# Gathers paced by their own landings instead of by pair products and mixes, in a recommendation tower on one core

## The reference

```python
e = jnp.stack([tbl_0[ids[:, 0]], ..., tbl_25[ids[:, 25]]], axis=1)
x = layer_norm(dense_t @ Wd.T, gd, bd)
y = layer_norm(jnp.einsum('bnd,ed->bne', sparse_t, Ws), gs, bs)
y = jnp.einsum('bne,pn->bep', y, Wsi)
y = layer_norm(y, gsi, bsi)
y = jnp.swapaxes(y, 1, 2)
T = jnp.concatenate([x[:, None, :], y], axis=1)
Z = jnp.einsum('bnd,bmd->bnm', T, T)
Zflat = Z[:, TRIL_I, TRIL_J]
out = layer_norm(Zflat @ Wl.T, gl, bl)
h = jnp.concatenate([z, r_dense_t], axis=1)
h = jnp.maximum(h @ W_top1 + b_top1, 0.0)
h = jnp.maximum(h @ W_top2 + b_top2, 0.0)
y = h @ W_top3
```

## Time and profile before

| | us |
|---|---|
| runs (3), median | 211.37 |
| runs, lowest to highest | 209.83 to 212.67 |
| the profiled execution's own time | 211.83 |
| its span, first to last instruction | 210.0 |

### The profile page before, as it was taken

One profiled execution on the slowest core, in us unless ns is written; L12 is line 12 of the kernel. 1 busy time (PEld: TensorE's weight loads), 2 busy tenths in 40 slices (PEclk: granted clock), 3 DMA queues, 4 the chain that ended last, 5 costly groups with the idle time before them and its releaser, 6 DMA issues.

```text
span 210.0 us, 4185 instructions
## 1 busy us (share of the span) xinstructions
PE 162.5 (77%) x1644; PEld 105.3 (50%) x1644; DVE 99.3 (47%) x192; ACT 88.5 (42%) x225; POOL 100.0 (48%) x113
## 2 busy tenths in 40 slices
PE   0593888683798795948986878579877969997996
PEld 0332635351355363726554637355555567465574
DVE  2463928635457655553072738260545574661011
ACT  2613235451164664541473436232644535642251
POOL 4777374667474664765546557736173710000000
PEclk9999589999599998596999999958999978999999
DMA  6713314172011144111101243101010630005100
GB/s 160 229 21 79 108 29 112 33 246 53 16 25 18 29 118 76 28 26 21 25 6 30 81 91 53 28 16 27 4 28 13 153 50 3 0 3 138 24 3 0
DMA packets 20260, 11.58 MB, mean 55 GB/s; under 512 B 12945, under 2 KB 17681, under 8 KB 20242
## 3 DMA queue, kind: packets, MB, share of 16 engines
q1 hardware_dynamic: 16226, 7.83, 14.2%
q0 software_dynamic: 3328, 3.41, 8.6%
q10 hardware_dynamic: 688, 0.08, 0.3%
HBM read 9.15 MB, written 2.16 MB: 54 GB/s over the span
## 4 chain that ended last, share of the span: by engine, by line
PE 63%; issue 19%; DVE 10%; DMA 4%; ACT 3%; SPq 0%; ACTq 0%; DVEq 0%
PE proj_ps L474 11%; PE mix_ps L440 10%; PE o_ps L490 8%; PE quad_ps L451 7%; PE dots_ps L465 6%; PE o_turn_ps L403 3%; PE o_turn_ps L528 2%; DVE var_p L881 2%; PE turn_ps L432 2%; PE o_ps L403 2%; DVE feats L905 2%; DVE e_prod L890 2%; DVE var_n L893 2%; PE o_ps L422 2%; PE dots_ps L396 2%
## 5 line engine op out<-in xcount | busy, mean ns | idle before, releaser
L373 POOL DMA_INDIRECT e_rows<-table_dram,rows_sb x104 | 99.1, 953 | 68.1 <-PE dots_ps L465 33.8
L890 DVE TENSOR_TENSOR e_prod<-quad_ps,e_rows 128x384 f32<-128x384 f32 (+1 forms) x16 | 9.5, 591 | 56.6 <-PE quad_ps L451 44.7
L465 PE MATMUL dots_ps<-feats 128*32 128x33 f32 x1024 | 19.1, 203 | 21.2 <-issue 20.8
L474 PE MATMUL proj_ps<-f_sb,proj_w 128*128 128x512 f32 x60 | 32.2, 619 | 1.3 <-DVE feats L905 0.6
L465 PEld LDWEIGHTS dots_ps<-feats 128*32 128x32 f32 x1024 | 14.6, 113 | 36.1 <-issue 35.0
L440 PE MATMUL mix_ps<-mixw_sb,e_unit 128*128 128x192 f32 (+4 forms) x128 | 26.7, 364 | 6.3 <-issue 5.1
L440 PEld LDWEIGHTS mix_ps<-mixw_sb,e_unit 128*128 128x128 f32 x128 | 24.8, 235 | 13.6 <-issue 9.9
L682 ACT COPY f_sb<-mix_ps 64x512 f32<-64x512 f32 x32 | 18.5, 579 | 20.1 <-PE mix_ps L440 16.4
L490 PE MATMUL o_ps<-wl_gained,z_pairs 128*128 128x512 f32 (+1 forms) x40 | 21.2, 664 | 0.5 <-DMA z_pairs<-z_dram 0.5
L451 PEld LDWEIGHTS quad_ps<-gram,e_cols 128*128 128x128 f32 x104 | 13.4, 194 | 16.3 <-issue 11.0
L881 DVE TENSOR_REDUCE var_p<-y_sq 128x16 f32<-128x512 f32 x32 | 20.5, 677 | 1.6 <-ACT y_sq L667 1.6
(11 more groups left out here) (142 smaller groups left out, 176.8 us busy)
## 6 DMA issues: line engine op xcount, KB each, us to landing
z_dram<-z_mine SPq DMA_DIRECT2D x4, 512.0 KB, 3.2
e_rows<-table_dram,rows_sb POOLq DMA_INDIRECT x104
w_sb<-w_dram SPq DMA_DIRECT2D x2, 512.0 KB
wl_sb<-wl_dram SPq DMA_DIRECT2D x2, 512.0 KB
w_sb<-w_dram SPq DMA_DIRECT2D x1, 768.0 KB
dense_sb<-dense_t_dram SPq DMA_DIRECT2D x1, 512.0 KB
wl_sb<-wl_dram SPq DMA_DIRECT2D x1, 256.0 KB
z_pairs<-z_dram SPq DMA_DIRECT2D x4, 64.0 KB, 2.1
```

The source lines that it names most:

```text
L373: pool.indirect_dma_start(out=e_rows[:, chunk, t, D * ab:D * (ab + 1)], out_offset=None, in_=table, in_offset=bass.IndirectOffsetOnAxis(ap ...
L465: mm = pe.matmul(dots_ps[PR * k:PR * (k + 1), (PR + 1) * g:(PR + 1) * (g + 1)], f[:, 2:PR + 2], f[:, 0:PR + 1], start=True, stop=True)
L474: pe.matmul(proj_of(s, ab), proj_w[:], f_sb[:, q % 2, ab, :], start=True, stop=True).then_inc(projected, 1)
L890: dve.tensor_tensor(e_prod[:, 0:2 * nt, :].rearrange("p a d -> p (a d)"), quad_ps[:, 0:P * nt], e_rows[:, chunk, t0:t0 + nt, :].rearrange( ...
```

## The change

The sixteen semaphores `gathered` are replaced by four, `landed`, that the gathers increment in turn: gather g (0 to 103) adds 16 to `landed[g % 4]` when it lands. Before gather g is issued, POOL waits until gather g-3 has landed, so that at most three are in flight. POOL waits for nothing else: `after_round` is gone, with its waits for `mixed`, `dotted` and earlier rows. Who needs a slot's rows (`turn` on PE, the four loads on SP) waits for all four semaphores to reach the count of that slot's last gather. DVE's wait in `variance_n` is dropped; it waits for `quad_done` there in any case.

```diff
+IN_FLIGHT = 3
+
+
+def gathers_up_to(s):
+
+    return sum(2 * tiles_of(slot % QUARTERS)[1] for slot in range(s + 1))
...
-        gathered = [[sem(f"gathered{chunk}_{q}") for q in range(QUARTERS)] for chunk in range(CHUNKS)]
+        landed = [sem(f"landed{k}") for k in range(IN_FLIGHT + 1)]
...
+        def rows_landed(eng, s):
+
+            number = gathers_up_to(s)
+            for k in range(IN_FLIGHT + 1):
+                eng.wait_ge(landed[k], 16 * ((number - 1 - k) // (IN_FLIGHT + 1) + 1))
...
             for q in range(3):
-                sp.wait_ge(gathered[0][q], 32 * tiles_of(q)[1])
+                rows_landed(sp, q)
...
-            sp.wait_ge(gathered[0][3], 32 * tiles_of(3)[1])
+            rows_landed(sp, 3)
...
-            def after_round(i):
-                if i >= 2:
-                    pool.wait_ge(dotted, i - 1)
-                elif i >= 0:
-                    pool.wait_ge(mixed, i + 1)
-                    pool.wait_ge(gathered[0][i + 1], 32 * tiles_of(i + 1)[1])
-
-            for chunk in range(CHUNKS):
-                for q in range(QUARTERS):
-                    after_round(chunk * QUARTERS + q - 2)
-                    t0, nt = tiles_of(q)
-                    for t in range(t0, t0 + nt):
-                        for ab in range(2):
-                            col = (chunk * TILES + t) * 2 + ab
-                            pool.indirect_dma_start(
...
-                            ).then_inc(gathered[chunk][q], 16)
+            for s in range(SLOTS):
+                chunk, q = place(s)
+                t0, nt = tiles_of(q)
+                for n in range(2 * nt):
+                    g = gathers_up_to(s) - 2 * nt + n
+                    if g >= IN_FLIGHT:
+                        older = g - IN_FLIGHT
+                        pool.wait_ge(landed[older % (IN_FLIGHT + 1)], 16 * (older // (IN_FLIGHT + 1) + 1))
+                    t, ab = t0 + n // 2, n % 2
+                    col = (chunk * TILES + t) * 2 + ab
+                    pool.indirect_dma_start(
...
+                    ).then_inc(landed[g % (IN_FLIGHT + 1)], 16)
...
-                pe.wait_ge(gathered[chunk][q], 32 * nt)
+                rows_landed(pe, s)
...
-                dve.wait_ge(gathered[chunk][q], 32 * nt)
```

More of the change, by code:

```diff
@@ L357, in _ @@
             pool.wait_ge(rows_ready, 1)
-            def after_round(i):
-                if i >= 2:
-                    pool.wait_ge(dotted, i - 1)
-                elif i >= 0:
-                    pool.wait_ge(mixed, i + 1)
-                    pool.wait_ge(gathered[0][i + 1], 32 * tiles_of(i + 1)[1])
-            for chunk in range(CHUNKS):
-                for q in range(QUARTERS):
-                    after_round(chunk * QUARTERS + q - 2)
-                    t0, nt = tiles_of(q)
-                    for t in range(t0, t0 + nt):
-                        for ab in range(2):
-                            col = (chunk * TILES + t) * 2 + ab
-                            pool.indirect_dma_start(
-                                out=e_rows[:, chunk, t, D * ab:D * (ab + 1)], out_offset=None, in_=table,
-                                in_offset=bass.IndirectOffsetOnAxis(ap=rows_sb[:, col:col + 1], axis=0),
-                            ).then_inc(gathered[chunk][q], 16)
+            for s in range(SLOTS):
[9 more added lines that the diff above has]
+                    pool.indirect_dma_start(
+                        out=e_rows[:, chunk, t, D * ab:D * (ab + 1)], out_offset=None, in_=table,
+                        in_offset=bass.IndirectOffsetOnAxis(ap=rows_sb[:, col:col + 1], axis=0),
+                    ).then_inc(landed[g % (IN_FLIGHT + 1)], 16)
         @block.tensor
```

## The result

The changed kernel takes **285.21 us** (median of 4 runs, 284.60 to 285.66), the kernel before 210.60 (4 runs, 209.75 to 212.67). The ratio is **1.352, with a 95% interval of 1.341 to 1.364**: 74.6 us slower, where 269 us was forecast with a range of 218 to 291. The profiled execution took 284.60 us with a span of 282.8. One thing for reading the runs further down: some executions come out 1.5 to 4% longer than the shortest of their kernel (three of four in e1, and of the kernel before two of seven beside e5 to e8 and five of seven beside e9 to e11), and e1 and the ratios are read from the others.

What follows compares the result with a forecast made beforehand. PE was taken to bound the kernel, stalling for instructions during gather bursts. Gathers landed at 135.1 us plus 132.0 us of rest gave 267.1 us of span, with 1.8 us more 269 us (+27%); range 218 to 291 us.

Steps and rivals of the forecast that it cites:

- starving as in the sum: Main case: unbroken gathers keep PE short of instructions until 135.1 us; 269 us, own range 240 to 291, chance 0.69.
- The landing wait costs nothing: On POOL, 101 gathers wait for the gather three back; about 1.4 us of slack, so cost 0.
- The stall ends with the burst, 1.41 us behind it: PE's stall in `dots` ends when the burst's last rows land; the stream's last gather ends at 133.7, landed at 135.1 us.
- The trickle of 1.76 records per us: While gathers stream, PE runs 1.76 records per us, the longest stall's rate: 239 records when the gathers end.
- The stock of some 59: PE holds some 59 records, hardly refilled while gathers are in flight, and spends them by 33.1 us.
- The rest without gathers: After the gathers the remaining work takes 132.0 us: 151.0 less 15 for later stalls and 4 for the clock.
- Four semaphores at `turn`: PE's `turn` waits on four semaphores instead of one, 17 more wait instructions; cost taken as 0, at most 4.9 us.
- "Issue" in mixes and projections too: Sign of being right: PE nearly idle with "issue" before its records from about 33 us, not in `dots` alone.
- No stalled `dots` afterwards: Sign of being right: from about 135 us, without gathers, every `dots` step on PE takes 0.77 us.
- partial starving: Rival: PE's trickle of records grows in a long gather stream; 216 to 243 us, chance 0.14.
- Faster: Rival: a stream hurts `dots` steps no more than a burst, or only present bursts stall PE; some 204 us, chance 0.09.
- No change: Rival: landing waits space the gathers and PE is refilled in the gaps; 207 to 216 us, chance 0.08.

Runs made afterwards that it cites:

- e1: The changed kernel with the old `after_round` waits for mixes and pair products put back, landing waits and four semaphores kept: 205.95 us beside 206.32 to 208.05.
- e5: The kernel before without `after_round`, POOL memsets in place of the gathers of chunks 1 to 3, which reuse chunk 0's rows: 171.10 us beside 177.53.
- e8: The kernel before without `after_round`, with a 0.33 us POOL memset ahead of each gather from the ninth on: 192.44 us, ratio 1.083.
- e9: The changed kernel itself run again, on a third chip beside the kernel before: 285.12 us, ratio 1.369.
- e11: The kernel before without `after_round`, plain DMAs of fixed rows issued by POOL in place of the gathers of chunks 1 to 3: 184.37 us beside 211.10.
- e2: The kernel before without its `after_round` waits, sixteen semaphores kept and no landing waits: 282.75 us.
- e3: The changed kernel with one gather in flight instead of three: 338.17 us.
- e4: The kernel before with only chunk 0's 26 gathers, chunks 1 to 3 reading its rows again, so 78 gathers left out: 173.72 us, ratio 0.837.
- e10: The kernel before without `after_round`, a POOL memset ahead of each gather from the ninth on, as in e8 but on another chip: 265.38 us.
- e12: The kernel before without `after_round`, with one 1.50 us POOL memset ahead of every eighth gather: 264.46 us beside 210.22.
- the spaced stream: The kernel of e8 and e10, the kernel before without `after_round` and a memset ahead of each gather from the ninth on: 192.44 and 265.38 us.
- run 45: Not a run label: the words are part of "PE had run 45 records by 33.1 us", a count of PE's records in the changed kernel.

## Why the prediction was right, and where its steps were off

The sign and the size were right: starving as in the sum, 269 us forecast, 285.2 measured, inside the range. The mechanism, that gathers keep instructions from PE and that the rounds were what protected it, was right; e1, e2 and e11 show it. That it is instructions of which PE runs short is still a reading, since no view shows an instruction being fetched. One step behind the number failed and three terms were mis-sized. That they partly cancelled was luck.

**The landing wait costs nothing** (I took 0 by a slack of 1.4 us). It measured 6.3 us in three waits; 3.14 us of them at the fourth gather, while the inputs are being loaded. The stream ended at 139.46 instead of 133.7: **+5.8 us**. e2 has no such waits and ends its gathers at 134.50.

**The stall ends with the burst, 1.41 us behind it.** This is the step that failed. I read those 1.41 us, seen at slot 3, a burst of six, as the landing of the last rows, and let the stall end with them. Rows do land in about that time: in e3, with nothing piled up, POOL stands 1.7 us from the end of a gather to the start of the next, and 0.3 of them lie between any two gathers. But the landing does not end a stall; the two only came together after six gathers. By the reading it ends 1.40 us per gather after the burst's first one, which holds to 0.3 us at all eight stalls. The release came 12.7 us after the last gather and not 1.4: **+11.3 us**. The trace of before could have told the two apart: PE is released 1.33 to 1.46 us after the end of the last gather of six, but 1.67 to 1.71 after the last of eight, and the difference is 2 x 0.15. It showed the grid too, in the stall from 47.64 us:

```profile
48.76 0.20 PE L465 MATMUL dots_ps<-feats 128*32 128x33 f32 x1 [0.57 <-issue]
...
50.17 0.19 PE L465 MATMUL dots_ps<-feats 128*32 128x33 f32 x1 [1.21 <-issue]
...
50.90 0.19 PE L465 MATMUL dots_ps<-feats 128*32 128x33 f32 x1 [0.54 <-issue]
51.62 0.32 PE L465 MATMUL dots_ps<-feats 128*32 128x33 f32 x3 [0.53 <-issue]
...
54.46 0.47 PE L465 MATMUL dots_ps<-feats 128*32 128x33 f32 x14 [0.45 <-issue]
```

With the two that are not shown, at 53.03 and 53.76, the starts are 1.41, 0.73, 0.72, 1.41, 0.73 and 0.70 us apart. I had counted the records in this window and not looked at their spacing. Read with the 1.25 us between gathers, two steps per gather would have given a queue that grows by 0.15 us each time.

**The trickle of 1.76 records per us.** Mis-sized: from 33.1 to 134.8 us 116 - 45 = 71 records ran, 0.70 per us, and for 44 of those 102 us (11.1 + 10.2 + 23.0) PE waited for VectorE and ScalarE, of which the sum has nothing. The stall of 6.26 us was not "the nearest to a stream that never ends": a quarter of it lay behind its last gather, which ended at 52.79, where the queue empties. The 1.15 of all stalls was nearer, and still high. So PE stood at 126 records at the release instead of 239, where the kernel before is at 42.5 us, not 59.0: **+16.5 us**.

**The stock of some 59.** PE had run 45 records by 33.1 us, not 59, and 53 by 40 us, and then it waited for the other two engines. So the stream does not test the number. That PE has records ready it does show: 30 ran from 93.19 to 97.03, in the middle of the crawl. A refill in blocks explains the crawl no better. The Trainium skill ("Runtime: NRT & Kernel Launch", "Instruction fetch mechanics") has instruction refills in blocks on a DMA queue. The packets of that queue in 90 to 152 us of the changed kernel, over the crawl and its end:

```profile
q8 instruction: 1, 0.02, 0.1%
```

One packet, between 94 and 95 us, while PE ran its 30 records, and none near the release at 152 us. So PE went on record by record after a block had come, and was let go without a new one: a missing block explains neither the grid nor the release.

**The rest without gathers** (132.0 us, 151.0 less 15 for stalls and 4 for the clock). It measured 282.8 - 152.15 = 130.65, with 113 records more to run than forecast. Behind 42.5 us the kernel before takes 167.5, so the rest gave back 36.9 us, where I had 19: **-17.9 us**. e4 shows this term by itself, 129.3 us for the same stretch. Part of it goes with the term before: behind 42.5 us lies the longest stall too, 7.29 - 0.77 = 6.5 us. For the rest, I had priced only what stalls in `dots` steps, and gathers also lengthen the steps between.

Sum: 267.1 + 5.8 + 11.3 + 16.5 - 17.9 = 282.8, the span. So the forecast of the span was 16 us off, the 17.1 of the first two terms, because the two others of some 17 us stood against each other.

**The other terms.** Four semaphores at `turn`: within nothing, by e1. "Issue" in mixes and projections too: the label stands there, but PE waited for VectorE and ScalarE, whose own starving I had not forecast. No stalled `dots` afterwards: yes. Rivals: "partial starving" forecast a trickle that grows in a long stream; it shrinks instead. "Faster" rested on a stream that does no more harm than a burst; wrong on these chips, and with it what the Trainium skill's "DMA: Bandwidth & Descriptors", "Rules for kernel authors" would say here, to issue a DMA early and wait late. e2 is that rule followed to the letter, 282.75 us. "No change" needed gathers further apart; e10 has them a little, 1.44 us, at 265.

**What stays open.** What it is that a gather occupies for 1.40 us and that the instructions of PE, VectorE and ScalarE pass, the runs do not say. Nor why one chip of four in the batches does not have it; POOL's gathers take 0.94 to 0.95 us on both kinds. Every execution here comes with a span and a granted clock, so it was recorded. The prediction took the agreement of 211.83 and 211.37 as a sign that the stall is not the profiler's; it is none, if both were recorded. That the writing of the records is what the gathers collide with is a rival that no run tests, and it would make the whole effect one of profiled runs.

## What to carry to other kernels

Look at a stall's inner spacing and not only at its count. A regular grid, two steps of which are longer than the time between two issues of its cause, points to a queue, and a queue that a short burst hides grows with a long stream; here PE was let go 1.4 us behind six gathers, 1.7 behind eight and 12.7 behind 104. Before a wait is taken away because nobody needs it for its data, ask what else it paces: here POOL's waits for pair products kept indirect gathers from starving three other engines for longer than a burst; e1 adds waits at no cost that shows, e2 drops these and loses 36% (282.75 against 207.57). And compare versions on more than one chip: the spaced stream was 8% over the kernel before on one and, in a single run, some 26 to 28% on another.

## What the runs showed that I had not expected

- By the reading above, an indirect gather of 128 rows occupies 1.40 us of something shared on chips of the first kind, though POOL shows 0.94 us and the DMA share is small (0.15 from 93.1 to 97.1 us). Plain DMAs of 128 rows, 0.53 us apart, occupy nothing that shows (e11).
- The crawl outlasts its cause: 12.7 us after the last of 104 gathers (14.6 in e2, 12.3 in e9), 1.8 after 26 (e11), 2.4 after bursts of eight (e12) and 0.9 after a stream at 1.44 us (e10).
- It holds ACT and DVE as well as PE: a DVE instruction whose input was done at 94.8 ran at 115.12, and an ACT copy at 67.47 whose matmul was done at 53.3.
- Chips differ by more than the edit of an ordinary study: the kernel before took 177.5 us on one and 207.6 to 211.1 on three others, and without the 78 later gathers 171.1 (e5) and 173.7 (e4). So the difference between these two chips is nearly all in the gathers.
